# The alignment recurrence from both ends at once, in segments of 188 rows

## The reference, cut to what matters

```python
def _align_one(small, large):            # small: context, 1500 rows; large: normalized x, 56 rows
    D = _pairwise_euclidean(small, large)        # 1500 x 56
    R = _dtw_cost(D)   # R[i,j] = D[i,j] + min(R[i-1,j], R[i,j-1], R[i-1,j-1])
    i_idx, j_idx, valid = _backtrack(R, T_small, T_large)   # from the last cell: diagonal, up or left,
                                                            # whichever is least, to (0, 0)
    contrib = small[i_idx] * valid[:, None]
    return zeros.at[j_idx].add(contrib)  # for each token, the sum of the context rows on its path
x = x + jnp.tanh(g_xattn[0]) * vmap(_align_one)(ctx_1024, _layernorm(x))
...
```

## Time and profile before

| | |
|---|---|
| median of 3 runs | 528.3 us |
| the profiled execution | 530.6 us, of it the span 528.8 |
| TensorE busy (matmuls) | 431.2 us, 82% |
| VectorE busy | 377.7 us, 71% |
| ScalarE busy | 262.5 us, 50% |
| GpSimd busy | 86.8 us, 16% |
| mean granted clock of TensorE | 0.948 |
| chain that ended last | TensorE 46%, VectorE 35%, issue 8%, GpSimd 7% |

### The profile page before, as it was taken

One profiled execution on the slowest core, in us unless ns is written; L12 is line 12 of the kernel. 1 busy time (PEld: TensorE's weight loads), 2 busy tenths in 40 slices (PEclk: granted clock), 3 DMA queues, 4 the chain that ended last, 5 costly groups with the idle time before them and its releaser, 6 DMA issues.

```text
span 528.8 us, 10186 instructions
## 1 busy us (share of the span) xinstructions
PE 431.2 (82%) x4021; PEld 254.3 (48%) x4021; DVE 377.7 (71%) x995; ACT 262.5 (50%) x454; POOL 86.8 (16%) x101
## 2 busy tenths in 40 slices
PE   9997778758888887101778899999999999989996
PEld 7444333326655573000334456666666666544444
DVE  8668999998666786865685888988979883371112
ACT  4565888655322691100102456666656567634443
POOL 1000000001000005787980000210210211100000
PEclk9999999898999999655798999999999999999999
DMA  8600674325513005963180004384384491000000
GB/s 285 226 0 23 183 213 137 109 89 152 149 58 91 28 2 126 231 150 87 36 175 1 0 1 106 74 176 103 77 177 94 84 285 37 2 1 0 0 1 17
DMA packets 28719, 50.06 MB, mean 95 GB/s; under 512 B 2464, under 2 KB 18400, under 8 KB 28672
## 3 DMA queue, kind: packets, MB, share of 16 engines
q1 hardware_dynamic: 26848, 45.74, 32.3%
q0 software_dynamic: 1536, 3.67, 2.7%
q10 hardware_dynamic: 288, 0.00, 0.0%
HBM read 39.96 MB, written 9.45 MB: 93 GB/s over the span
## 4 chain that ended last, share of the span: by engine, by line
PE 46%; DVE 35%; issue 8%; POOL 7%; ACT 3%; DMA 1%; DVEq 0%; POOLq 0%
PE banks L1626 7%; PE banks L1602 7%; POOL arena L548 6%; PE banks L1657 5%; DVE arena L1230 4%; DVE work L1259 4%; PE banks L1704 4%; DVE mx L1033 4%; PE banks L1718 4%; DVE arena L1283 2%; DVE mx L1041 2%; PE banks L1470 2%; PE banks L1316 2%; DVE work L1225 2%; PE banks L1320 2%
## 5 line engine op out<-in xcount | busy, mean ns | idle before, releaser
L1033 DVE TENSOR_REDUCE mx<-banks 112x1 f32<-112x500 f32 x168 | 106.9, 676 | 18.2 <-PE banks L1602 18.2
L778 ACT ACTIVATE arena<-banks 128x896 f32<-128x896 f32 x96 | 87.9, 917 | 49.9 <-PE banks L1657 49.2
L1340 PE MATMUL banks<-steps,one 128*128 128x500 f16 (+1 forms) x201 | 56.5, 376 | 33.8 <-DVE hcol L981 33.8
L1626 PE MATMUL banks<-arena 128*32 128x112 f32 (+1 forms) x1536 | 58.1, 265 | 3.4 <-issue 2.5
L1602 PE MATMUL banks<-ctxT,arena 128*112 128x500 bf16 x144 | 54.7, 393 | 3.7 <-DVE mx L1041 1.1
L1626 PEld LDWEIGHTS banks<-arena 128*32 128x32 f32 (+1 forms) x1536 | 33.9, 109 | 23.7 <-issue 21.0
L1340 PEld LDWEIGHTS banks<-steps,one 128*128 128x128 f16 x201 | 20.3, 103 | 48.7 <-issue 38.2
L1259 DVE SCALAR_TENSOR_TENSOR work<-twice,banks,arena 128x202 f32<-128x202 f32 x68 | 29.5, 434 | 18.8 <-PE banks L1470 18.8
L1657 PEld LDWEIGHTS banks<-arena,ctxT 128*128 128x128 bf16 (+1 forms) x576 | 37.3, 104 | 9.7 <-issue 1.9
L1657 PE MATMUL banks<-arena,ctxT 128*128 128x112 bf16 (+1 forms) x576 | 40.9, 213 | 0.0
L548 POOL DMA_INDIRECT arena<-in_w_tab,idx x32 | 34.6, 1082 | 11.6 <-issue 9.5
(11 more groups left out here) (264 smaller groups left out, 773.1 us busy)
## 6 DMA issues: line engine op xcount, KB each, us to landing
ctxT<-key_parts SPq DMA_DIRECT2D x36, 375.0 KB, 6.4
key_parts<-arena SPq DMA_DIRECT2D x32, 281.2 KB, 2.9
ctxT<-in_ctx_T SPq DMA_DIRECT2D x12, 500.0 KB, 8.8
arena<-key_parts SPq DMA_DIRECT2D x12, 375.0 KB, 7.9
ctxT<-in_ctx_nat SPq DMA_DIRECT2D x5, 750.0 KB
arena<-in_ctx_nat SPq DMA_DIRECT2D x3, 750.0 KB
arena<-in_L_ffn_W SPq DMA_DIRECT2D x1, 2048.0 KB, 10.0
arena<-in_fold_w SPq DMA_DIRECT2D x1, 768.0 KB, 5.8
```

Of the source, the lines that this page charges most:

```text
L778: nc.scalar.activation(Pt[0:rows, g % 2, :].rearrange("p (a n) -> p a n", a=2), banks[0:rows, 2 + 2 * (g % 2):4 + 2 * (g % 2), 0:HQ // 2], ...
L1033: nc.vector.tensor_reduce(mx3[:, b % 2, u // NPIECE, u % NPIECE:u % NPIECE + 1], ps[k % 2][0:2 * NJ, 0:PIECE], AX_X, ALU.max).then_inc(s_m ...
L1340: nc.tensor.matmul(bank[:, 0:cols], one16[:, :], steps16[:, 0:cols], start=True, stop=True, skip_group_check=True)
L1626: last = nc.tensor.matmul(ps[6 + b % 2][q:q + 32, o:o + 2 * NJ], vals[0:rows, v0:v0 + 32], Pt[0:rows, g % 2, 2 * t * NJ:2 * (t + 1) * NJ], ...
```

## The change

The recurrence runs forward over the first 28 columns and, in other lanes, backward from the last cell over the other 28. For that the 1500 rows are padded to 1504 = 8 segments of 188, and the lanes are 2 directions x 8 batches x 8 segments (LB = NS = 8, NG = 16). STEPS is 28 + 8 - 1 = 35, a block is TB = 2 steps, NTB = 18.

- A unit of the distance phase is DU = 376 rows of two batches from the start and, read backwards, 376 from the end: four products and four norm matmuls, each 32 columns wide (JP); UN = 16. Loads: eight of the two ends, four of the middle; the squares are kept for the whole context instead of in a ring.
- The scan reads the distances in PSUM; `lane_distances` is gone. `turn` has four pieces of 94 rows, `dist_of` two activations.
- Keys: 24 steps of 500 columns; the blocks have 2, 2, 1 of them in turn. The stores' ring has 6 places instead of 8.
- GpSimd gathers the forward lanes' last column from the last eight steps (13 operations); VectorE adds the last piece.
- Between recurrence and walk the halves are joined: TensorE turns the backward column to the forward lanes (`turned`), VectorE adds it, takes the least per lane and its place, TensorE brings lane minima into one row, VectorE takes the least per batch, TensorE spreads the row to all lanes of both halves (`begin`), and `begin16` puts it into the hops' bank where a lane starts.
- The walk goes 34 hops back from the crossing, both halves at once; `twice` has 378 elements, EARLY_VALUES is 8, and the warming matmul is gone from the loop.
- 64 masks (16 slabs of 94 rows, 4 pairs of batches) instead of 60.

```diff
+    HJ = NJ // 2
+    NG = 2 * NB
+    LB = P // NG
+    PADU = 2
+    NS = LB
+    C = (NI + 2 * PADU) // NS
+    STEPS = HJ + NS - 1
...
-    TB = 5
+    TB = 2
-    STORES = 8
-    EARLY_VALUES = 16
+    STORES = 6
+    EARLY_VALUES = 8
-    KPIECE = 375
+    KPIECE = 500
-    KEYS_OF_CHUNK = [0, 1] + 7 * [3] + 5 * [2]
+    KEYS_OF_CHUNK = [0, 0, 0] + 4 * [2, 2, 1] + [2, 2, 0]
...
+            pool.wait_ge(s_blk, 1)
+            for s in range(NS - 1):
+                pool.wait_ge(s_scan, HJ + s)
+                nc.gpsimd.tensor_tensor((cross1 if s else cross), view(R, [[1, SLOT]], (HJ + s) * SLOT),
+                                        segment[:, s:s + 1].broadcast_to([P, SLOT]), ALU.mult).then_inc(s_cross, 1)
+                if s:
+                    pool.wait_ge(s_cross, 2 * s)
+                    nc.gpsimd.tensor_tensor(cross, cross, cross1, ALU.add).then_inc(s_cross, 1)
+                    pool.wait_ge(s_cross, 2 * s + 1)
...
             def dist_of(u):
-                nc.scalar.activation(view(dist[:, :], [[JW, SPP], [BS, 2], [1, NJ]], ...), ..., ACT.Sqrt
-                                     ).then_inc(s_dist, 1)
+                for k in range(2):
+                    last = nc.scalar.activation(view(dist[:, :], [[NB * BS, 4], [BS, 2], [1, HJ]], ...), ..., ACT.Sqrt)
+                last.then_inc(s_dist, 1)
...
-            def lane_distances(q):
-                act.wait_ge(s_dt, q + 1)
...
-                d = dts[:, (t % (2 * DT_STEPS)) * C:(t % (2 * DT_STEPS) + 1) * C]
-                nc.vector.tensor_tensor_scan(view(R, [[1, C]], (t + 1) * SLOT + 1), m, d,
+                nc.vector.tensor_tensor_scan(view(R, [[1, C]], (t + 1) * SLOT + 1), m,
+                                             ps[t // TB % 2][:, t % TB * C:(t % TB + 1) * C],
...
+            ve.wait_ge(s_cross, 2 * NS - 3)
+            nc.vector.scalar_tensor_tensor(out=cross, in0=view(R, [[1, SLOT]], STEPS * SLOT),
+                                           scalar=segment[:, NS - 1:NS], in1=cross, op0=ALU.mult, op1=ALU.add
+                                           ).then_inc(s_crossed, 1)
+            jump_inputs(NCODES - 1)
+            rows_not_left(NCODES - 2)
+            ve.wait_ge(s_back, 1)
...
+            rows_not_left(NCODES - 1)
+            jump_targets(NCODES - 3)
+            ve.wait_ge(s_lowrow, 1)
...
+            jump_targets(NCODES - 2)
+            ve.wait_ge(s_spread, 1)
+            link(nc.vector.scalar_tensor_tensor(out=filled[:, :], in0=limit[:, :], scalar=ps[0][:, 384:385],
+                                                in1=ps[0][:, 384:384 + NF + 1], op0=ALU.is_gt, op1=ALU.mult))
+            nc.vector.tensor_tensor(begin16[:, :], filled[:, 1:NF + 1], filled[:, 0:NF], ALU.subtract
+                                    ).then_inc(s_inject, 1)
+            jump_targets(NCODES - 1)
...
             def dots(u):
-                for h in range(2):
-                    nc.tensor.matmul(ps[4 + u % 2][h * J64:(h + 1) * J64, 0:PIECE], xm2[:, 2 * g + h, :],
-                                     piece(ctxT, u)[:, h, :], start=True, stop=False, skip_group_check=True)
+                for k in range(4):
+                    nc.tensor.matmul(ps[4 + u % 2][k * JP:(k + 1) * JP, lo:hi], xm2[:, g, k // 2, k % 2, :],
+                                     along(ctxT[:, :], u, k), start=True, stop=False, skip_group_check=True)
...
+            key_step(NKP)
+            jump_codes(NTB - 3)
+            pe.wait_ge(s_crossed, 1)
+            nc.tensor.matmul(ps[0][0:P // 2, 0:SLOT], turned[:, :], view(cross, [[-1, SLOT]], C), start=True, stop=True
+                             ).then_inc(s_back, 1)
+            jump_codes(NTB - 2)
...
                 nc.tensor.matmul(ps[2][:, t - 1:t], blk16[:, :], acc[:, t - 1:t], ...).then_inc(s_hop, 1)
-                keep_busy(ps[3], 1, 384)
```

More of the change, by code:

```diff
@@ L96, in build_gated_layers @@
     N0 = len(PAIR_COLS)
-    CODES = [(k * TB, TB) for k in range(NTB - 1)] + [(STEPS - TB, TB - 1), (STEPS - 1, 1)]
+    CODES = [(t, min(TB, STEPS - t)) for t in range(0, STEPS, TB)]
     NCODES = len(CODES)
@@ L141, in build_gated_layers @@
         R = arena[:, o_R:]
+        M_RING = 2 * TB
+        assert M_RING * C <= 2 * N_B and TB * C <= N_B
         mring = work[:, 0:2 * N_B]
-        dts = work[:, 2 * N_B:4 * N_B]
-        rise = [work[:, (4 + a) * N_B:(5 + a) * N_B] for a in range(2)]
[L146 to L149, removed]
@@ new lines, in build_gated_layers @@
+        rises = [work[:, o_rises + a * HB:o_rises + (a + 1) * HB].bitcast(F16) for a in range(2)]
+        rise = [work[:, (4 + a) * N_B:(5 + a) * N_B] for a in range(2)]
+        left = [work[:, 6 * N_B + a * HB:6 * N_B + (a + 1) * HB].bitcast(F16) for a in range(3)]
+        never = [work[:, 6 * N_B + a * HB:6 * N_B + (a + 1) * HB].bitcast(F16) for a in range(3, 5)]
+        assert 5 * HB <= 2 * N_B and 5 * SLOT <= 2 * N_B
+        back, least, total, place, chosen = [work[0:P // 2, o_xn + a * SLOT:o_xn + (a + 1) * SLOT] for a in range(5)]
@@ new lines, in _ @@
+            nc.vector.tensor_tensor(least[:, 0:C], backp, back[:, 1:SLOT], ALU.min)
+            link(nc.vector.tensor_tensor(chosen[:, 0:C], back[:, 1:SLOT], backp, ALU.is_le))
+            nc.vector.tensor_tensor(total[:, 0:C], cross[0:P // 2, 1:SLOT], least[:, 0:C], ALU.add)
+            link(nc.vector.scalar_tensor_tensor(out=place[:, 0:C], in0=chosen[:, 0:C], scalar=-NEVER,
+                                                in1=view(twice[0:P // 2, :], [[2, C]], 2), op0=ALU.add, op1=ALU.add))
@@ new lines, in _ @@
+            nc.vector.tensor_copy(zall[:, 1:FROM + 1], ps[2][:, 0:FROM])
+            link(nc.vector.tensor_tensor(zall[:, FROM + 1:], ps[2][:, FROM:STEPS], filled[:, 0:NF], ALU.add))
+            for a in range(2):
+                rows = zall[:, :] if a == 0 else view(zall[:, :], [[-1, ZW]], STEPS)
+                last = nc.vector.tensor_tensor(
+                    zt[:, :, a, :], rows.unsqueeze(1).broadcast_to([P, NB, ZW]),
+                    first3[:, :, a].unsqueeze(2).broadcast_to([P, NB, ZW]), ALU.mult)
@@ L1350, in query_norms @@
                 pe.wait_ge(s_xn2, g + 1)
[L1351 to L1352 removed]
+                nc.tensor.matmul(ps[NORM_BANK[g]][:, g:g + 1], xn2[:, g, :], quarter[:, :], start=True, stop=True
+                                 ).then_inc(s_bb, 1)
             pe.wait_ge(s_mw, 1)
@@ L1437, in _ @@
             pe.wait_ge(s_dist, UN)
-            lane_columns(2)
+            lane_columns(3)
             keys_of(0)
-            key_step(0)
-            lane_columns(3)
-            for k in range(2, NTB):
+            jump_codes(0)
+            for k in range(3, NTB):
+                if k + 1 < NTB:
+                    lane_columns(k + 1)
                 for i in KEY_STEPS[k]:
```

456 lines of the change are left out of this document (252 added, 204 removed).

## The result

The changed kernel takes 561.2 us, median of 4 runs (560.87 to 561.4), beside 529.04 us for the kernel before on the same chip: a ratio of 1.0601, with an interval of 1.0567 to 1.0634. It is 6% slower, where the forecast was 500 us and the range ended at 514. The profiled execution took 561.4 us, with a span of 559.7 against 528.8.

What follows compares the result with a forecast made beforehand. VectorE's throughput was taken to bound the recurrence, a chain of VectorE and TensorE the walk. Terms -20.2 + 1.0 + 6.4 - 19.1 + 1.4 + 2 = -28.5 us, giving 500 us, range 492 to 514.

Steps and rivals of the forecast that it cites:

- moves as a whole: Behind the masks: this work doesn't depend on how the path was found and keeps its length, its loads being in place.
- I cost this at nothing: Recurrence: ScalarE (3.8 us) and TensorE (3.6) keep up with a 3.95 us block, so no cost; the cover is thin.
- distance phase: Before the recurrence: 16 units of 2.03 us instead of 12 of 2.51, copy gone, later turns: +1.0 us.
- recurrence, with GpSimd's +2: Recurrence: fewer, longer columns on VectorE, -20.2 us; GpSimd's thirteen operations beside VectorE, +2.
- tail: Last scan to first search: joining the halves in series takes 10.6 us instead of 4.15, +6.4.
- walk: Walk back: 34 searches of 0.90 us instead of 69, 30.6 against 49.7 us, -19.1.
- (c): Distance phase: quarter-width matmuls run only in pairs, or reversed operands at half rate; +18 us, 518; chance 0.08.
- (e): Distance phase: quarter-width matmuls run one after the other; +60 us on the forecast, 560; chance 0.02.
- the price list: Recurrence: VectorE prices per column and extra work that add up to a block, giving 3.95 us for two columns.
- rival (b): Recurrence: the key pipeline sets the block, ten two-key blocks at 4.7 us instead of 3.95; +7.5, 507; chance 0.15.
- rival (d): Walk: TensorE sets it, a hop taking 1.4 us at its lower clock; +17 us, 517; chance 0.05.
- a bound of 7.8: Last seven columns of the recurrence: most that thirteen GpSimd operations could cost VectorE, 13 x 0.6 us; full blocking chance 0.08.

Runs made afterwards that it cites:

- only_late: Changed kernel with 96 rows in the six context loads issued behind the recurrence, 94 in the two inside it: 523.64 us, ratio 0.9894 to the kernel before.
- only_recurrence: Changed kernel with 96 rows in the two context loads issued during the recurrence, 94 in the six others: 541.03 us, ratio 1.0199 to the kernel before.
- rows96: Changed kernel with all eight context loads over 96 rows instead of 94, two of them unread zeros: 505.1 us, ratio 0.9519 to the kernel before.
- before94: Kernel before the change, each of its eight 100-row context loads cut into 94 and 6 rows: 565.65 us, ratio 1.0665.
- rows_mixed: Changed kernel with a row count for each batch's context load (112, 95, 98, 94, 99, 100, 104, 96): 509.37 us, one run.
- half_rows: Changed kernel, each 94-row context load cut into two halves with rows of 4096 bytes: 564.73 us, ratio 1.0627 to the kernel before.

## Why the prediction was wrong

**The step that failed** is a sentence under what bounds the kernel: everything behind the masks "moves as a whole, as the loads that it needs are long in place". They were long in place in the kernel before. In the changed one the last of them arrives 32 us after the masks end (190.50 to 222.56), and what waits for it, sums and all behind them, loses 37 us (1.0601 against 0.9894, only_late): 30.7 of waiting, and matmuls that ran longer at the lower granted clock. I read the diff for instructions of the compute engines and took a load of the same bytes for the same load; the sum has no term for the eight loads, and the row count of 94 was in the diff.

**A second step failed with it**: "I cost this at nothing", of what must keep up in the recurrence. I had checked ScalarE and TensorE against a block of 3.95 us and not the stores behind them. The early loads hold two DMA engines for 15 us each, each key store that follows has a part on those two, so it lands 17 to 18 us after its issue instead of 3, and the buffer it is stored from comes free that much later; ScalarE's activation, the jump codes and VectorE's scan then stand behind it: 21 us (only_recurrence). That the path runs through the store is what the chain shows (17.96 and 16.96 us). That the stores stand behind the load on those two engines is in the times of landing of the kernel after. The early load landed at 81.9 and 82.3 us. Of the store issued at 65.55, 14 parts landed at 67.9 to 70.0 and the other two at 83.1 and 83.5; of the next three, 14 parts each had landed by 71.1, 75.7 and 81.7, and the other two only at 84.2 and 84.6, at 85.4 and 85.8, and at 86.5 and 87.0. Windows on either side of the load's end:

```profile
75.50:79.00 3.50, 0.00 (x0) 0.00 (x0) 2.75 (x9) 0.00 (x0) 0.00 (x0) 0.73 0.13 54
82.00:85.50 3.50, 1.18 (x4) 0.53 (x5) 0.00 (x0) 1.91 (x4) 0.00 (x0) 0.50 0.14 42
```

The share is that of two engines in both: first the load, then what it had held up of the stores.

The cause, the number of engines, is shown by rows96 (the loss gone with two more rows), before94 (the loss in a kernel without the change) and rows_mixed (shares, and times of landing for eight row counts). The Trainium skill (DMA: Bandwidth & Descriptors, section "Why a DMA increments its semaphore by 16 and not by 1") states the rule: the engines used are the largest number up to 16 that divides the size of the slowest dimension on both sides, with 100 rows giving 10. This case's traces agree: a share of 0.58 to 0.65 and ten times of landing for 100 rows, 0.13 and two for 94.

**The rest of the sum held.** Without the slow loads (rows96 against the earlier trace rows):

| term | forecast | measured |
|---|---|---|
| distance phase | +1.0 | 47.35 - 45.5 = +1.9 |
| recurrence, with GpSimd's +2 | -18.2 | 58.45 - 76.10 = -17.7 |
| tail | +6.4 | 11.46 - (125.75 - 121.6) = +7.3 |
| walk | -19.1 | 31.67 - 49.71 = -18.0 |
| masks and sums | +1.4 | 24.77 - 22.94 = +1.8 |
| sum | -28.5 | -24.7 up to there, -26.1 over the span |

Each term came out a little worse than forecast, and none by more than 1.1 us. Distance phase: the timeline of TensorE after, one unit and the next, beside the earlier trace rows:

```profile
28.00 0.84 PE L1426 MATMUL banks<-ctxT,work 128*32 128x376 f32 x8
28.66 0.81 PE L1431 MATMUL banks<-arena,ones 128*32 128x376 f32 x8
29.40 0.64 PE L1443 MATMUL banks<-ident,arena 128*94 128x128 f32 x4
29.97 0.84 PE L1426 MATMUL banks<-ctxT,work 128*32 128x376 f32 x8
```

The products and the norms of a unit take 0.66 and 0.74, the unit 1.97 where I had 2.03 (every fourth unit takes 2.4). What looks mis-sized is the hand-over at the end, put at 1.4 us to the good: in rows96 the scan of step 6, at 47.35, waits 2.03 us for TensorE, where before the scan at 45.47 waited 1.35 for ScalarE's copy. Rivals (c) and (e) are out: quarters run side by side, and with half of the operands read backwards the group of four takes no longer than one such matmul was priced at (0.65). That (e) had 560 us and the kernel took 561 is chance. Recurrence: the timeline of VectorE after, one block before any stall:

```profile
48.83 0.35 DVE L1297 TENSOR_TENSOR work<-arena 128x188 f32<-128x188 f32 x1
...
49.29 0.61 DVE L1301 TENSOR_TENSOR_SCAN arena<-work,arena,banks 128x188 f32<-128x188 f32 x1
...
52.77 0.35 DVE L1297 TENSOR_TENSOR work<-arena 128x188 f32<-128x188 f32 x1
```

From 48.83 to 52.77 is 3.94 us, forecast 3.95; the price list held. The key pipeline (rival (b)) doesn't set the block: rows96 has no wait of the scan at L1287. The stretch lost 0.5 us against the forecast. Tail: 11.5 us where I had 10.6. The copy of the turned column starts 4.8 us after the last scan (110.59 in rows96, behind a wait of 2.46) instead of 3.6; the wait was foreseen, but not all of it; and the rest of the tail is 0.3 shorter than forecast. Walk: searches are 0.90 apart as forecast (136.66, 137.56, 138.46), but three stand further apart: 1.29, 1.07 and 1.40. The timeline of VectorE after shows the first of them, and a window of the kernel after lies over all three:

```profile
138.46 0.62 DVE L1363 SCALAR_TENSOR_TENSOR work<-twice,banks,arena 128x378 f32<-128x378 f32 x1 [0.27 <-PE banks L1588]
...
139.75 0.62 DVE L1363 SCALAR_TENSOR_TENSOR work<-twice,banks,arena 128x378 f32<-128x378 f32 x1 [0.66 <-PE banks L1588]
```

```profile
138.50:141.90 3.40, 3.40 (x18) 3.31 (x18) 1.85 (x6) 1.10 (x3) 0.00 (x0) 0.50 0.13 53
```

Behind a tail in which TensorE was busy 7.00 of 11.36 us, its granted clock is 0.50 for these 3.4 us, the lower of the two levels (1.2 GHz); it is 1.00 from 142 us to the end of the walk, with the searches 0.90 to 0.91 apart. That is rival (d)'s mechanism over three hops instead of all: 1.1 us, not 17.

## What to carry to other kernels

When a tiling changes, look at the row count of every transfer that takes its shape from it, and not at its bytes alone: here 94 rows went over 2 DMA engines and 96 over 16, and that outweighed 26 us won in the compute. A load with slack is not safe at any speed: ask what it costs at a fraction of its rate, and which stores are queued behind it. A share of DMA that stays flat at a small fraction, with something moving all the while, is the mark of it in a profile.

## What the runs showed of the hardware

- Rows and DMA engines, by the times of landing of a load: 94 rows 2 (share of DMA 0.13, 52 to 56 GB/s), 95 rows 5 (7.3 us), 99 rows 11, 100 rows 10 (share 0.58 to 0.65), 104 rows 13, 98 rows 14, 96 and 112 rows 16. The size of the rows played no part: half_rows was no faster.
- A transfer issued behind one on two engines waits for it on those two alone: 14 of a key store's 16 parts landed within 5 us of its issue, the other two 17.5 and 18 us after it, when the 94-row load was through.
- VectorE's two-input work beside GpSimd: single instructions of 0.54 us became 0.85, and of 0.35 became 0.67, each by 0.31 or 0.32. The Trainium skill (SBUF — State Buffer, section "SBUF: two separate sides") has one of the two engines blocked while the other works. The lengthened instructions agree with it in kind; but only some were met, so the price was 1.9 us of a bound of 7.8.
- Four 32-column f32 matmuls of 376 columns, on quarters of the array, were gone in 0.66 us, and an operand read backwards cost nothing that the trace shows.
